# Sorted experts of a four-layer kernel: first weights stationary, fetched per tile by SyncE, and the share applied by VectorE

## The reference, cut to what matters

```python
# layer 1 (E=8, K=2, F=512, exact gelu)
top_w, top_idx = jax.lax.top_k(w, K)
top_w = top_w / (top_w.sum(axis=-1, keepdims=True) + EPS_GATE)
for e in range(num_experts):
    h = jax.nn.gelu(xf @ W1[e] + b1[e], approximate=False)
    y = h @ W2[e] + b2[e]
    out = out + cw[:, e:e + 1] * y
# layer 2 (the same experts, but each takes at most 1.25 * tokens / E rows)
h = jax.nn.gelu(jnp.einsum('ecd,edf->ecf', buf, w1) + b1[:, None, :], approximate=False)
out = jnp.einsum('ecf,efd->ecd', h, w2) + b2[:, None, :]
y = jnp.zeros((n, d), x.dtype).at[tok].add(w[:, None] * og)
```

## Time and profile before

| | |
|---|---|
| median of 3 runs | 3429.66 us (3428.36 to 3429.71) |
| profiled execution | 3428.99 us, its span 3427.3 us |
| PE matmul busy | 2855.8 us (83% of the span) |
| PE weight loads busy | 1283.5 us (37%) |
| DVE busy | 2250.8 us (66%) |
| ACT busy | 1836.3 us (54%) |
| POOL busy | 1553.5 us (45%) |

### The profile page before, as it was taken

The page is one execution under the profiler, slowest core; times in us unless marked ns, Lnnn a source line. Parts: engine busy times, 40 slices in busy tenths (PEclk is TensorE's granted clock), DMA queues, the critical chain, the costliest instruction groups (busy, mean ns, idle before and its releaser), DMA issues. The chain is left out here.

```text
span 3427.3 us, 66581 instructions
## 1 busy us (share of the span) xinstructions
PE 2855.8 (83%) x21143; PEld 1283.5 (37%) x21144; DVE 2250.8 (66%) x3360; ACT 1836.3 (54%) x2941; POOL 1553.5 (45%) x1224
## 2 busy tenths in 40 slices
PE   3999999999999996799955599999978932574994
PEld 1333333333333335533323122222226622353772
DVE  5666666666666644788886799999944348525663
ACT  1555555555555550254463499999974443235432
POOL 0899999999999996100000001111115626450000
PEclk9999999999999997899976699999999965796995
DMA  2111111111111114500004222222221160113001
GB/s 86 32 43 48 42 57 42 48 42 57 42 48 42 57 40 149 163 1 1 0 2 139 56 56 52 58 49 56 56 90 41 46 194 30 31 44 94 11 13 55
DMA packets 263893, 189.54 MB, mean 55 GB/s; under 512 B 148174, under 2 KB 209990, under 8 KB 262576
## 3 DMA queue, kind: packets, MB, share of 16 engines
q1 hardware_dynamic: 255568, 174.05, 17.6%
q0 software_dynamic: 8224, 14.24, 1.3%
HBM read 105.21 MB, written 67.55 MB: 50 GB/s over the span
## 5 line engine op out<-in xcount | busy, mean ns | idle before, releaser
L542 DVE TENSOR_REDUCE attn_half_max<-attn_peek 128x2 f32<-128x1024 f32 x512 | 627.6, 1226 | 463.8 <-PE attn_peek L381 460.0
L330 POOL TENSOR_TENSOR attn_esum<-attn_esum,attn_prob 128x1024 f32<-128x1024 f32 x384 | 904.6, 2356 | 27.9 <-ACT attn_prob L481 1.9
L481 ACT ACTIVATE attn_prob<-attn_score 128x1024 f32<-128x1024 f32 x512 | 512.6, 1022 | 297.0 <-PE attn_score L364 297.0
L836 ACT ACTIVATE attn_prob<-attn_score 128x512 f32<-128x512 f32 x1024 | 556.3, 596 | 72.5 <-PE attn_score L786 58.2
L853 DVE TENSOR_REDUCE attn_half_max<-attn_peek 128x2 f32<-128x1024 f32 x512 | 583.4, 1214 | 10.9 <-PE attn_peek L772 10.9
L411 PE MATMUL attn_acc<-attn_prob,attn_v 128*64 128x512 f32 x2048 | 487.9, 597 | 0.1
L802 PE MATMUL attn_acc<-attn_prob,attn_v 128*32 128x256 f32 x4096 | 328.3, 392 | 12.0 <-ACT attn_out L828 10.5
L1733 POOL DMA_INDIRECT sorted_x<-attn_sent_rows,attn_send x64 | 62.5, 977 | 554.9 <-PE attn_score L786 520.1
L772 PE MATMUL attn_peek<-attn_ke,attn_qe 48*128 48x512 bf16 x1024 | 203.1, 394 | 45.2 <-DMA attn_ke<-k 30.3
L381 PE MATMUL attn_peek<-attn_hi 64*128 64x512 f16 x1024 | 199.8, 387 | 14.8 <-DVE attn_half_max L542 14.8
L411 PEld LDWEIGHTS attn_acc<-attn_prob,attn_v 128*64 128x64 f32 x2048 | 130.8, 137 | 207.1 <-issue 162.4
(11 more groups left out here) (531 smaller groups left out, 4467.5 us busy)
## 6 DMA issues: line engine op xcount, KB each, us to landing
attn_xb<-attn_x_all SPq DMA_DIRECT2D x66, 256.0 KB, 2.5
attn_invB<-inv SPq DMA_DIRECT2D x64, 256.0 KB, 3.9
o<-attn_out SPq DMA_DIRECT2D x32, 512.0 KB
out_o<-o SPq DMA_DIRECT2D x8, 2048.0 KB
mix_f<-picked SPq DMA_DIRECT2D x16, 512.0 KB, 7.3
experts_x<-sorted_x SPq DMA_DIRECT2D x112, 65.0 KB
attn_qe<-q SPq DMA_DIRECT2D x192, 32.0 KB
attn_ke<-k SPq DMA_DIRECT2D x192, 32.0 KB
```

What stands on the lines that cost most here:

```text
L330: nc.gpsimd.tensor_tensor(own, before, prob[:, u % NPROB, :, :], ALU.add).then_inc(added, 1)
L481: nc.scalar.activation(prob[:, u % NPROB, :, :], score[:, u % 2, :, :], ACT.Exp).then_inc(exped, 1)
L542: V.tensor_reduce(half_max[:, :, t, half], peek[:], AX.X, ALU.max, negate=True).then_inc(maxed, 1)
L836: nc.scalar.activation(prob[:, n % NPROB, :], score[:, n % RING, :], ACT.Exp).then_inc(exped, 1)
```

## The change

What it does, part by part, in `sorted_experts_stage`:

1. `project` swaps the operands: the four 128-column pieces of w1 are stationary and xT moves, in four matmuls with 128 columns each. The hidden rows come out turned, so `turn_h`, `hid`, `ht` and the copy of hidT on ACT are gone: gelu writes `hidT` directly, and `down` waits for gelu.
2. w1 no longer lies in SBUF for all experts. SP reads the tile's expert from the table, and loads that expert's w1 (128 x 512, 256 KB) into one of four buffers, when `project` of four tiles before is done. PE then needs no register for `project`. The loads of w1 and b1 during the attention and in `mix1` are gone.
3. b1 is needed down the partitions: 32 x 128 values are loaded, turned by one matmul at the start of the stage and copied by DVE. `add_bias` adds it spread along the columns.
4. The share is applied by DVE: `finish` first computes b2 * share (a TENSOR_SCALAR), then out * share + that (a SCALAR_TENSOR_TENSOR). POOL's multiplication is gone.

```diff
@@ class ExpertWeights
-    LOADS = 3
+    LOADS = 1
...
-        sp.dma_start(self.w1[:, own], w1_d[bass.ds(e, 1)].rearrange("a d f -> d (a f)")).then_inc(loaded, DMA)
-        sp.dma_start(self.b1[:, own], broadcast_rows(b1_d.rearrange("e f -> (e f)")[own])).then_inc(loaded, DMA)
@@ sync
             sp.dma_start(b2[:], broadcast_rows(weights.weights_d[3].rearrange("e d -> (e d)"))).then_inc(consts, DMA)
+            sp.dma_start(raw_b1[:], weights.weights_d[1].rearrange("e (k p) -> (e k) p", p=P)).then_inc(consts, DMA)
...
+            def load_w1(n, u, first=False):
+                e = expert_of(sp, n)
+                if not first:
+                    sp.wait_ge(projected, n - UNROLL + 1)
+                sp.dma_start(w1[:, u, :], w1_d[bass.ds(e, 1)].rearrange("a d f -> d (a f)")).then_inc(w1_in[u], DMA)
+
+            sp.wait_ge(consts, NCONST * DMA)
+            for n in range(UNROLL):
+                load_w1(n, n, True)
+            AHEAD = 3 if job else 2
             if job:
                 job.load(sp)
             for l in range(1, AHEAD):
                 for u in range(UNROLL):
+                    load_x(UNROLL * l + u, u)
+                    if l > 1 or u > 0:
+                        load_w1(UNROLL * l + u - 1, (u - 1) % UNROLL)
+                if l == 1 and job:
                     job.spread(sp)
             with sp.Fori(AHEAD, NL) as l:
                 for u in range(UNROLL):
+                    load_x(UNROLL * l + u, u)
+                    load_w1(UNROLL * l + u - 1, (u - 1) % UNROLL)
+            load_w1(blocks - 1, UNROLL - 1)
@@ gpsimd, send
                 pool.wait_ge(y_ready, n + 1)
-                nc.gpsimd.tensor_scalar(y[:, n, :], y[:, n, :], result[:, n, 1:2].bitcast(F32), None, ALU.mult).then_inc(shared, 1)
-                pool.wait_ge(shared, n + 1)
@@ tensor
-            def project(n, s, any_before):
-                e = expert_of(pe, n)
+            def project(n, u, any_before):
+                s = u % 2
                 pe.wait_ge(x_copied, n + 1)
+                pe.wait_ge(w1_in[u], DMA * ((n - u) // UNROLL + 1))
                 if any_before:
                     pe.wait_ge(biased, n - 1)
-                mm(up[:, s, :], xT[:, s, :], w1[:, bass.ds(e * F, F)], start=True, stop=True).then_inc(projected, 1)
-
-            def turn_h(n, s, any_before):
...
                 for k in range(FT):
-                    last = nc.tensor.transpose(ht[:, s, k * P:(k + 1) * P], hid[:, s, k * P:(k + 1) * P], ident[:])
-                last.then_inc(h_turned, 1)
+                    last = mm(up[:, s, k * P:(k + 1) * P], w1[:, u, k * P:(k + 1) * P], xT[:, s, :], start=True, stop=True)
+                last.then_inc(projected, 1)
 
             def down(n, s, any_before):
                 e = expert_of(pe, n)
-                pe.wait_ge(h_copied, n + 1)
+                pe.wait_ge(gelu_done, n + 1)
@@ scalar, body
-                nc.scalar.activation(hid[:, s, :], pre[:, s, :], ACT.Gelu).then_inc(gelu_done, 1)
+                nc.scalar.activation(hidT[:, s, :], pre[:, s, :], ACT.Gelu).then_inc(gelu_done, 1)
...
-                nc.scalar.activation(hidT[:, s, :], ht[:, s, :], ACT.Copy).then_inc(h_copied, 1)
@@ vector
-                V.tensor_tensor(pre[:, s, :], up[:, s, :], b1[:, bass.ds(e * F, F)], ALU.add).then_inc(biased, 1)
+                V.tensor_tensor(pre[:, s, :].rearrange("p (k r) -> p k r", k=FT), up[:, s, :].rearrange("p (k r) -> p k r", k=FT),
+                                b1[:, bass.ds(e * FT, FT)].unsqueeze(2).to_broadcast([P, FT, P]), ALU.add).then_inc(biased, 1)
 
             def finish(n, s):
                 e = expert_of(dve, n)
+                dve.wait_ge(kept, n + 1)
+                share = result[:, bass.ds(n, 1), 1:2].rearrange("p a b -> p (a b)").bitcast(F32)
+                V.tensor_scalar(b2_share[:, s, :], b2[:, bass.ds(e * D, D)], share, None, ALU.mult).then_inc(b2_ready, 1)
                 dve.wait_ge(summed, n + 1)
-                V.tensor_tensor(y[:, bass.ds(n, 1), :].rearrange("p a d -> p (a d)"), out[:, s, 0:D], b2[:, bass.ds(e * D, D)],
-                                ALU.add).then_inc(y_ready, 1)
+                dve.wait_ge(b2_ready, n + 1)
+                V.scalar_tensor_tensor(out=y[:, bass.ds(n, 1), :].rearrange("p a d -> p (a d)"), in0=out[:, s, 0:D], scalar=share,
+                                       in1=b2_share[:, s, :], op0=ALU.mult, op1=ALU.add).then_inc(y_ready, 1)
```

More of the change, by code:

```diff
@@ L1823, in sorted_experts_stage @@
         result = st.sb("result", [P, blocks, 2], I32)
-        w1, b1, w2 = weights.w1, weights.b1, weights.w2
+        w1_d, w2 = weights.weights_d[0], weights.w2
+        raw_b1, b1 = st.sb("raw_b1", [E * FT, P]), st.sb("b1", [P, E * FT])
+        w1 = st.sb("w1", [P, UNROLL, F])
         b2 = st.sb("b2", [P, E * D])
@@ L1856, in iterations, with expert_of @@
                 body(blocks - UNROLL + u, u, False, True)
+        def expert_of(eng, n):
+            return eng.value_load(expert[0:1, bass.ds(n, 1)], min_val=0, max_val=E - 1)
         @block.sync
@@ L1861, in _, with load_x @@
             sp.dma_start(b2[:], broadcast_rows(weights.weights_d[3].rearrange("e d -> (e d)"))).then_inc(consts, DMA)
+            sp.dma_start(raw_b1[:], weights.weights_d[1].rearrange("e (k p) -> (e k) p", p=P)).then_inc(consts, DMA)
             for n in range(UNROLL):
                 sp.dma_start(x[:, n, :], xs_d[n * P:(n + 1) * P, :]).then_inc(loaded[n], DMA)
-            AHEAD = 3 if job else 1
+            def load_x(n, u):
+                sp.wait_ge(x_turned, n - UNROLL + 1)
+                sp.wait_ge(kept, n - UNROLL + 1)
+                sp.dma_start(x[:, u, :], xs_d[bass.ds(n * P, P), :]).then_inc(loaded[u], DMA)
+            def load_w1(n, u, first=False):
[7 more added lines that the diff above has]
+            AHEAD = 3 if job else 2
             if job:
@@ L1900, in _ @@
             pool.wait_ge(stored, DMA * blocks)
-        def expert_of(eng, n):
-            return eng.value_load(expert[0:1, bass.ds(n, 1)], min_val=0, max_val=E - 1)
         @block.tensor
@@ L1945, in body @@
                 if not (final and u == UNROLL - 1):
-                    project(n + 1, 1 - s, not (first and u == 0))
-                turn_h(n, s, not (first and u < 2))
+                    project(n + 1, (u + 1) % UNROLL, not (first and u == 0))
                 if not (first and u == 0):
@@ L1951, in _ @@
             pe.wait_ge(consts, NCONST * DMA)
+            nc.tensor.transpose(out[:, 0, 0:E * FT], raw_b1[:], ident[0:E * FT, 0:E * FT]).then_inc(b1_turned, 1)
             turn_x(0, 0, False)
@@ L1976, in body @@
                 if not (first and u < 2):
-                    act.wait_ge(h_turned, n - 1)
-                nc.scalar.activation(hid[:, s, :], pre[:, s, :], ACT.Gelu).then_inc(gelu_done, 1)
+                    act.wait_ge(summed, n - 1)
+                nc.scalar.activation(hidT[:, s, :], pre[:, s, :], ACT.Gelu).then_inc(gelu_done, 1)
                 if not (final and u >= UNROLL - 2):
                     copy_x(n + 2, s, True)
-                act.wait_ge(h_turned, n + 1)
-                if not (first and u < 2):
-                    act.wait_ge(summed, n - 1)
-                nc.scalar.activation(hidT[:, s, :], ht[:, s, :], ACT.Copy).then_inc(h_copied, 1)
             copy_x(0, 0, False)
@@ L2012, in body @@
                     finish(n - 1, 1 - s)
-            dve.wait_ge(consts, NCONST * DMA)
+            dve.wait_ge(b1_turned, 1)
+            V.tensor_copy(b1[:], out[:, 0, 0:E * FT]).then_inc(b1_ready, 1)
+            dve.wait_ge(b1_ready, 1)
             add_bias(0, 0, False)
```

38 lines of the change are left out of this document (12 added, 26 removed).

## The result

The changed kernel takes **3407.49 us** (median of 4 runs, 3404.78 to 3413.20) against 3429.68 us before: a ratio of 0.9938, 95% interval 0.9921 to 0.9955. It is 22 us faster where 52 were forecast, and lies 1.5 us above the range. The profiled execution took 3410.15 us, its span 3408.4.

What follows compares the result with a forecast made beforehand. PE's queue was taken as the bound; at 2.25 us per tile, 51.4 us gained in steady stretches, less 7 at starts, plus 7.8 at ends, made 52 us, so a median of 3378 us, range 3352 to 3406.

Steps and rivals of the forecast that it cites:

- What bounds the kernel before: Expert stages before the change: PE's queue is the bound, one register load with what follows 0.7 us or more, twice per tile.
- DVE 2.25 us: Changed expert tile: DVE's two register loads, TENSOR_SCALAR, semaphore and branch take 2.25 us (2.15 to 2.35), setting the pace.
- 0.06 for the semaphore (estimate): Term in DVE's time per tile, added behind the TENSOR_SCALAR's 0.25 us: 0.06 us.
- PE 2.2 and POOL 2.1: Changed expert tile: PE's queue with branch takes 2.2 us, POOL without its multiplication 2.1 us.
- SP or transfers at 2.5 us: Rival, expert tiles: SP's queue or the w1 transfers become the bound at 2.5 us per tile, 3402 us; chance 0.17.
- Array alone, 2.05 us: Rival, expert tiles: PE's array alone sets the pace at 2.05 us per tile, 3359 us; chance 0.12.
- Weight loads not hidden: Rival, `project`: its eight weight loads stand alone, 1.5 us in place of 0.9, 2.6 per tile, 3411 us; chance 0.03.
- Slower, DVE behind POOL's scatter: Rival, b2 * share on DVE: cannot start during a scatter, losing up to 1.03 us per tile, 3478 us; chance 0.05.
- Starts and ends: Both expert stages: first bias 3 us later each, -6; ends 3.9 us shorter each, 7.8 gained.
- The spreading of the reciprocal: Start of experts1: job's loads stand behind four w1 issues, tiles 7 and 8 wait longer: -1 us more (0 to -5).

Runs made afterwards that it cites:

- before_pe_entry: The kernel before the change, with TensorE (PE) loading the expert's register once more in `down`; 3496.18 us.
- one_pe: one_entry with one more load of the expert's register on PE, in `down`; 3413.36 us.
- one_entry: Changed kernel with b2 * share computed a tile ahead, behind the bias addition, into four buffers, and DVE's second register load per tile gone; 3348.68 us.
- no_w1: Changed kernel without any w1 fetches after the first four of each stage, nor their register loads and waits; 3401.66 us.
- share_pool: Changed kernel with only part 4 undone: POOL multiplies y by share again, DVE adds b2 as before; 3417.95 us.
- two_ahead: one_entry with DVE's second register load put back in `finish`, to no use; 3379.49 us.

## Why the prediction was off

*What bounds the kernel before: right.* PE's queue, 0.6 to 0.7 us per load; before_pe_entry measured 0.63.

*DVE 2.25 us: the step that failed.* Its mechanism was named (the second load, then the TENSOR_SCALAR), its size was not right. The sum's terms against the means over the 58 intervals: from last operation to bias, with the branch, 0.95 + 0.1 = 1.05, measured 1.12; from bias to TENSOR_SCALAR 1.85 - 0.95 = 0.90, measured 0.92; from there to the last operation 0.25 + 0.06 = 0.31, measured 0.50. So 2.26 was 2.54, and two thirds of the 0.28 us are in the last term: the TENSOR_SCALAR took 0.286 for my 0.25, and "0.06 for the semaphore (estimate)" was 0.21, the gap between its end and the last operation. The shortfall of the steady stretches is 25.0 us over 97 intervals, 0.26 each. With DVE, PE and POOL forecast at 2.25, 2.2 and 2.1, tenths of a microsecond decided which of them sets the time.

*PE 2.2 and POOL 2.1: too high.* Measured 1.88 to 1.95 (one_pe less a load) for PE, and POOL kept up with 1.91 in one_entry. Neither showed, because DVE was slower. With PE at 2.2, one_entry would have gained some 28 us less (97 x 0.29).

*Rivals.* SP or transfers at 2.5 us: the time is near (3402 against 3407), the cause is not it (no_w1 left the tile at 2.46). Array alone, 2.05 us: not the change, but one_entry gets there and below, to 1.91. Weight loads not hidden: refuted, `project`'s eight pass in 0.97 us on PEld, and the array was full with them. By the Trainium skill, "TensorE: Matmul & The Clock Gate", section on the back-to-back issue gap, a matmul of 128 columns costs 81 ns and one of 512 costs 131; in that ratio `project` would have taken 2.4 us (estimate). The trace does not agree: 0.97 us.

*Slower, DVE behind POOL's scatter:* it exists, but small. In the change 83 of 112 TENSOR_SCALARs start inside a scatter; 72 keep 0.29 us, 4 take 0.30 to 0.35, 7 take about 0.5. All of those seven end 0.05 us behind the scatter's end. From one_pe:

```profile
2700.48 0.98 POOL L1906 DMA_INDIRECT picked<-experts_y,experts_result  x1 [1.19 <-DVE experts_y L2011]
...
2700.95 0.55 DVE L2005 TENSOR_SCALAR experts_b_share<-experts_b,experts_result 128x128 f32 x1
```

*Starts and ends.* 3 us each were forecast for the starts, 2.3 and 2.8 came; 3.9 each for the ends, 2.9 and 3.5 came. *The spreading of the reciprocal*, "-1 us more (0 to -5)", was -7.0, the second step that failed: I had counted only its later issue, and not 3 MB of w1 in the stretch in which the job brings 4 MB, nor a clock that falls in the waits. Without the later fetches (no_w1) 3.4 of the 7.0 come back; the clock falls there too.

## What to carry to other kernels

Where an engine's queue was the bound, one register load more cost 0.6 us (0.61 on DVE, 0.63 on PE). Whether a load hides depends on what the engine still has to work off: put the operation that needs the register right behind the one that loaded it, and a load behind a long operation, not in front of a short one. Moving work off a bound engine pays only down to the next engine's turn, so write each engine's turn out before and after, and look for the edit that lowers all of them: here the same change with one load less, and b2 * share a tile ahead, gained 81 us in place of 22. Work on an engine that isn't the bound can cost nothing per tile and still lengthen the end of a stage: POOL's multiplication, 13.7 us in share_pool. A transfer that is covered in the steady stretch can still collide with other traffic at the start of a stage.

## What was not expected of the hardware

The array took the 17 float32 records of a tile (two per product, one for the turn) in 1.89 us, 0.111 each, with no gap in 80 us, at a granted clock of 1.00 (2.4 GHz). A scatter held up DVE's TENSOR_SCALAR only if that was still at work some 0.2 us before the scatter's end: begun more than 0.51 us before the end it took its 0.28, begun 0.25 to 0.51 before, it was drawn out to 0.05 us behind the end (in the change, one_entry, one_pe and two_ahead alike, but for one of 0.34 in two_ahead that began 0.72 before). So it cost 0.28 us at most. In mix1 it was the scatter that grew. By the Trainium skill, "SBUF — State Buffer", section "Who interferes with whom", the two engines share one port pair, and a DVE operation that uses both of its port pairs, as a TENSOR_SCALAR can, is kept out for the whole instruction of GpSimd if that started first. Here most TENSOR_SCALARs that begin inside a scatter are not delayed, and in one_entry most also end inside it. So either the scatter does not hold the pair for its whole length, or this TENSOR_SCALAR does not need it; no run here tells which, and the few that are drawn out fit neither fully.
